# Attention kernel, first attention: score matmuls of 63 and 64 rows, a new step order, and the output norm on ScalarE

## The reference, cut to what matters

```
x: (8, 512, 256) float32; 16 heads of 16; layer norm at its end, no gain or bias
qkv = x @ w_qkv + b_qkv                 # q, k, v: (8, 16, 512, 16)
a = einsum('bhsd,bhtd->bhst', q, k)     # causal: later keys are -inf
a = softmax((a + mask) / sqrt(16))
z = einsum('bhst,bhtd->bhsd', a, v)     # back to (8, 512, 256)
y = layernorm(x + z @ w_out + b_out, eps=1e-5)
```

## Time and profile before

| | us |
|---|---|
| median of 3 runs | 2001.62 |
| lowest, highest run | 1996.41, 2005.23 |
| the profiled execution's own time | 1997.55 |
| its span, first to last instruction | 1996.0 |
| busy in the span: PE, DVE, ACT, POOL | 1787.4, 1109.8, 967.3, 934.7 |
| first attention, to its last matmul | 539.3 |
| of that: seven turns of the loop | 426.1 |

### The profile page before, as it was taken

How to read it: one execution, slowest core, us unless ns; L and a number is a source line. 1 busy time by engine, 2 the same in 40 slices (tenths; PEclk the granted TensorE clock), 3 DMA queues, 4 the chain that set the end, 5 groups by cost and what they waited for, 6 DMA issues and landing times. The chain is left out here.

```text
span 1996.0 us, 42845 instructions
## 1 busy us (share of the span) xinstructions
PE 1787.4 (90%) x14072; PEld 1353.2 (68%) x14072; DVE 1109.8 (56%) x2825; ACT 967.3 (48%) x1898; POOL 934.7 (47%) x923
## 2 busy tenths in 40 slices
PE   5899988898669999999979999599999999789887
PEld 3556655565347777777768888477777777577776
DVE  4566655666467766676523333676676666234343
ACT  2655545554336555555534444265555555333332
POOL 3355444554336655555423333455555555333433
PEclk7898888987779999999979999699999999799998
DMA  4333343334010000000121112100000001121221
GB/s 144 106 115 107 106 122 112 117 109 127 22 33 12 32 32 32 32 32 21 50 58 43 63 63 95 44 12 32 32 32 32 32 21 49 50 70 63 65 74 42
DMA packets 103736, 121.28 MB, mean 61 GB/s; under 512 B 23387, under 2 KB 75781, under 8 KB 103685
## 3 DMA queue, kind: packets, MB, share of 16 engines
q1 hardware_dynamic: 96772, 95.45, 15.7%
q0 software_dynamic: 6912, 25.17, 3.5%
HBM read 82.55 MB, written 37.77 MB: 60 GB/s over the span
## 5 line engine op out<-in xcount | busy, mean ns | idle before, releaser
L468 DVE TENSOR_REDUCE a_negm<-a_x 128x2 f32<-128x256 f32 (+3 forms) x256 | 202.4, 814 | 143.7 <-PE a_x L594 141.5
L430 ACT ACTIVATE a_PT<-a_c 128x384 f32<-128x384 f32 (+1 forms) x384 | 183.7, 522 | 139.7 <-PE a_c L633 84.4
L866 POOL TENSOR_TENSOR work<-work 128x512 f32<-128x512 f32 x128 | 164.5, 1287 | 152.2 <-DVE work L1016 151.0
L1541 DVE SCALAR_TENSOR_TENSOR m_hid<-m_a,mw_b,m_gate 128x512 f32<-128x512 f32 x96 | 71.9, 749 | 244.4 <-ACT m_gate L1479 219.8
L1034 DVE CUSTOM_DVE_ANT_0 l_x<-l_x,window 128x256 f32<-128x256 f32 (+1 forms) x512 | 184.1, 421 | 31.7 <-PE l_x L1131 31.7
L1065 PE MATMUL l_f<-w_hi,tails 128*128 128x512 f32 x384 | 168.8, 440 | 14.2 <-DVE work L1016 11.1
L949 ACT ACTIVATE l_PT<-l_c 128x512 f32<-128x512 f32 (+1 forms) x256 | 125.3, 542 | 87.8 <-PE l_c L1171 84.1
L1436 POOL TENSOR_TENSOR m_hid_lo<-m_hid,m_hid_hi 128x512 fp32r<-128x512 f32 x80 | 102.7, 1291 | 131.3 <-ACT m_hid_hi L1490 131.1
L1066 PE MATMUL l_f<-w_hi,tails 128*128 128x512 f32 x384 | 154.8, 403 | 0.0
L1067 PE MATMUL l_f<-w_lo,tails 128*128 128x512 f32 x384 | 154.1, 401 | 0.0
L880 POOL TENSOR_TENSOR l_PS<-l_PT 128x768 f32<-128x768 f32 x64 | 119.6, 1869 | 58.7 <-ACT l_PT L949 58.7
(11 more groups left out here) (240 smaller groups left out, 5091.8 us busy)
## 6 DMA issues: line engine op xcount, KB each, us to landing
a_Q<-qk_parts SPq DMA_DIRECT2D x192, 64.0 KB, 2.1
a_K<-qk_parts SPq DMA_DIRECT2D x192, 64.0 KB, 2.1
qk_parts<-a_qk_hi SPq DMA_DIRECT2D x32, 256.0 KB, 2.1
qk_parts<-a_qk_lo SPq DMA_DIRECT2D x32, 256.0 KB, 2.2
after_attn<-rows_out POOLq DMA_DIRECT2D x16, 512.0 KB, 5.2
xin<-after_attn SPq DMA_DIRECT2D x32, 256.0 KB, 3.1
m_xr<-after_attn SPq DMA_DIRECT2D x16, 512.0 KB, 4.1
xin<-in_L_attn_x SPq DMA_DIRECT2D x8, 512.0 KB, 3.5
```

The costliest lines, as they stand in the source:

```text
L430: nc.scalar.activation(PT[:, p // PG % 2, 2 * (p % PG) + hh, QOFF[t]:QOFF[t] + nq], SC[hh][:, 0:nq], ACT.Exp, scale=AD ** -0.5).then_inc(e ...
L468: dve.tensor_reduce(negm[:, q, 2 * p:2 * p + 2], MX[i % 2][:, :, 0:nk], AX.X, ALU.max, negate=True).then_inc(max_done, 1)
L866: pool.tensor_tensor(t1[:, par, w, :], t1[:, par, w, :], t2[:, par, w, :], ALU.add)\
```

## The change

1. Rows. The shift row of Q moves from partition 48 to 63 (and 127). The rows between are zero: DVE writes zeros once to 32 partitions at 32 and at 96 of Q, at the start. First-pass score matmuls (sm) read 63 rows in place of 48, second-pass ones (st) 64 in place of 49.
2. Order. STEPS is new. A turn begins at f_x; the three projections f_qk 0 to 2 stand in a row; sm 21 to 26, st 4 to 7 and ms 0 and 1 now belong to the f_ steps and so are done in the turn before (and, for sequence 0, ahead of the loop). The semaphore of the written parts is split in two, one for parts 0 and 1 and one for 2 and 3.
3. Banks. f_qk, mt, pv, f_v and out get new banks, and their waits are rewritten to match.
4. Norm. POOL makes, besides the power, minus the mean times the power (two small instructions more). ACT applies scale and bias in four instructions at step end, in the loop and in the last sequence; the four of POOL and DVE go. POOL keeps the store.

```diff
-        ODD, SLOTS = 64, 48
+        ODD, SHIFT = 64, 63
...
-        QK_IN = [FB[0], FB[1], FB[1], FB[1]]
-        MT_IN = [FB[0], FB[1], FB[0], FB[0]]
-        O_IN = [FB[0], FB[1], FB[1], FB[0]]
+        QK_IN = [FB[1], FB[0], FB[1], FB[0]]
+        MT_IN = [FB[1], FB[0], FB[0], FB[1]]
+        O_IN = [FB[0], FB[1], FB[0], FB[0]]
+        V_IN = [FB[1], FB[0], FB[1], FB[1]]
+        Y_IN = [FB[1], FB[0], FB[1], FB[0]]
...
+            f_x:0 f_xe:0 sm:27 st:8 mt:2 f_qk:0 f_qk:1 f_qk:2 f_qe:0 f_qe:1 f_qe:2 sm:28 st:9 ms:2 sm:29 sm:30
+            f_load:0 st:10 sm:31 st:11 pv:0 st:12 mt:3 ms:3 st:13 z0:0 f_load:1 z1:0 z2:0 f_qk:3 st:14 pv:1 f_sm:0
+            f_qe:3 st:15 ms:4 f_sm:1 f_sm:2 st:16 f_sm:3 st:17 f_sm:4 st:18 f_sm:5 f_load:2 f_sm:6 st:19 f_sm:7 ms:5
+            st:20 z0:1 st:21 f_sm:8 f_sm:9 st:22 z1:1 f_sm:10 f_sm:11 st:23 ms:6 pv:2 z3:0 z2:1 f_mt:0 z0:2 f_load:3
+            f_sm:12 ms:7 z1:2 f_sm:13 pv:3 z3:1 z0:3 z2:2 f_sm:14 f_sm:15 z3:2 f_v:0 z1:3 f_v:1 xr:0 f_v:2 f_st:0
+            f_sm:16 f_mt:1 z2:3 f_st:1 f_sm:17 f_sm:18 f_st:2 f_sm:19 z3:3 f_st:3 f_sm:20 out:0 out:1 out:2 out:3
+            f_sm:21 f_st:4 f_sm:22 f_st:5 f_sm:23 f_ms:0 f_ms:1 f_st:6 end:0 f_sm:24 f_v:3 f_sm:25 f_st:7 f_sm:26
...
-                            at = ODD * hh + SLOTS
+                            at = ODD * hh + SHIFT
...
                     elif name == "out" and i == TB - 1:
...
+                        pool.tensor_scalar(nb[:, :], mv[:, :, 0], -1.0, None, ALU.mult).then_inc(rstd_a, 1)
...
-                        for t in range(TB):
-                            pool.tensor_scalar(out[:, t, :], y[:, t, :], mv[:, t, 0:1], rs[:, t:t + 1],
-                                               ALU.subtract, ALU.mult).then_inc(out_done, 1)
+                        pool.tensor_tensor(nb[:, :], nb[:, :], rs[:, :], ALU.mult).then_inc(rstd_done, 1)
...
+                    elif name == "end":
+                        act.wait_ge(rstd_done, 2 * b + 2)
+                        act.wait_ge(stored, b * 16)
+                        for t in range(TB):
+                            nc.scalar.activation(out[:, t, :], y[:, t, :], ACT.Identity, scale=rs[:, t:t + 1],
+                                                 bias=nb[:, t:t + 1]).then_inc(out_done, 1)
...
+                            for at in (32, ODD + 32):
+                                dve.memset(Q[at:at + 32, :, 0:S].bitcast(F32), 0.0).then_inc(v_set, 1)
...
-                            rows = slice(ODD * hh, ODD * hh + SLOTS)
+                            rows = slice(ODD * hh, ODD * hh + SHIFT)
...
-                            rows = slice(ODD * hh, ODD * hh + SLOTS + 1)
+                            rows = slice(ODD * hh, ODD * hh + ODD)
```

More of the change, by code:

```diff
@@ L193, in first_attention @@
         lo_done, v_done, xhi_done, xlo_done = sem("lo_done"), sem("v_done"), sem("xhi_done"), sem("xlo_done")
-        parts_out = sem("parts_out")
+        parts_out = [sem(f"parts_out{n}") for n in range(2)]
         stacked = [sem(f"stacked{g}") for g in range(AG)]
@@ L216, in first_attention @@
         STEPS = [s.rsplit(":", 1) for s in """
[L217 to L223, removed]
+            f_x:0 f_xe:0 sm:27 st:8 mt:2 f_qk:0 f_qk:1 f_qk:2 f_qe:0 f_qe:1 f_qe:2 sm:28 st:9 ms:2 sm:29 sm:30
[4 more added lines that the diff above has]
+            f_sm:16 f_mt:1 z2:3 f_st:1 f_sm:17 f_sm:18 f_st:2 f_sm:19 z3:3 f_st:3 f_sm:20 out:0 out:1 out:2 out:3
+            f_sm:21 f_st:4 f_sm:22 f_st:5 f_sm:23 f_ms:0 f_ms:1 f_st:6 end:0 f_sm:24 f_v:3 f_sm:25 f_st:7 f_sm:26""".split()]
         STEPS = [(name, int(i)) for name, i in STEPS]
@@ L294, in tail @@
                     if (name, i) == FIRST_OF_LAST:
-                        sp.wait_ge(parts_out, NB * 128)
+                        for n in range(2):
+                            sp.wait_ge(parts_out[n], NB * 64)
                         sp.wait_ge(lo_done, NB * 4)
@@ L500, in do @@
                         dve.wait_ge(y_full, b * TB + i + 1)
-                        dve.tensor_tensor(y[:, i, :], FB[i % 2][:, 0:DM], xr[:, i, :], ALU.add)\
+                        dve.tensor_tensor(y[:, i, :], Y_IN[i][:, 0:DM], xr[:, i, :], ALU.add)\
                             .then_inc(y_done, 1)
@@ L513, in tail @@
                         ahead.low(dve, ahead_raw, ahead_wo, LOW.index((name, i)))
[L514 to L519, removed]
                 steps(dve, do, tail)
@@ L539, in do @@
                         for h in range(KT):
-                            if not isinstance(b, int):
-                                pe.wait_ge(front_free, b * NE - 1 + h)
+                            if not isinstance(b, int) and h == 0:
+                                pe.wait_ge(mrow_done, b * AG - 2)
                                 pe.wait_ge(y_done, b * TB - TB)
+                            elif not isinstance(b, int):
+                                pe.wait_ge(front_free, b * NE)
                             if isinstance(b, int):
@@ L553, in do @@
                         pe.wait_ge(xlo_done, b * KT + KT)
-                        if i > 1:
-                            pe.wait_ge(front_free, b * NE + i)
+                        if i == 1 and not isinstance(b, int):
+                            pe.wait_ge(mrow_done, b * AG - 1)
+                        elif i == 2:
+                            pe.wait_ge(front_free, b * NE + 1)
+                        elif i == 3:
+                            if isinstance(b, int):
+                                pe.wait_ge(front_free, 2)
+                            else:
+                                pe.wait_ge(o_free, b * AG - 3)
                         for h in range(KT):
```

76 lines of the change are left out of this document (39 added, 37 removed).

## The result

| | before | after |
|---|---|---|
| median of 5 runs, us | 2001.62 | 1985.24 |
| lowest, highest | 1996.41, 2005.23 | 1982.06, 1994.36 |
| profiled execution, its own time | 1997.55 | 1994.36 |
| first attention, to its last matmul | 539.3 | 532.7 |

The profiled execution of after happens to be the slowest of its five. A later profile of the same kernel (e5, 1986.46 us) has its last first-attention matmul 5 us earlier: one of its turns takes 58.5 us and not 61.4, and the stretch behind the last f_x is 2.3 us shorter. So what follows is read from places and waits, and sizes are taken from medians.

The account below looks back on a forecast made before the run. PE bounds each turn, with low clock and waits. Rows 4.2 plus removed waits 5.0 minus new waits 3.7 gives 5.5 us a turn, 38.5 in seven; with small terms -40, so 1958 us, range 1926 to 2000.

Parts of the forecast that it names:

- Rows: Score matmuls of the first attention: filled rows, even of zeros, keep PE's clock up, saving 4.2 us a turn.
- I let a fifth of the low time stay: Step in the rows term: some low clock remains after waits, so 5.3 us a turn saved becomes 4.2.
- the sign of being wrong on the rows: What would refute the rows term: score stretches at clock 0.50 with PE busy throughout.
- Waits removed: PE's waits in pv for POOL's masking and ACT's copy, and in the first score step for loads: 5.0 us a turn gone.
- Waits foreseen: New PE waits for ACT: 1.8 us a turn behind the three projections, 1.9 where turns meet, together 3.7.
- the seam: From the last out matmul to the next turn's first projection: PE waits 1.9 us a turn for ACT.
- "1 and 8": Lower and upper bound, in us a turn, on the new waits forecast at 3.7.
- (b): Rival: rows of zeros do nothing for the clock, only removed waits help, 2.1 us a turn: 1984 us, chance 0.15.
- (c): Rival: ACT stands in the norm step waiting for POOL's power, PE idles 5 us where turns meet: 2011 us, chance 0.08.
- (a): Rival: the clock stays up throughout and ACT's new waits are half, 8.5 us a turn saved: 1932 us, chance 0.18.
- the first reading of the prediction: Reading of the profile page: PEclk is 9 in local attention and feed-forward slices, 7 to 9 in the first eleven.
- (d): Rival: the parts of the change cancel without any other rival's mechanism: about 1996 us, chance 0.07.

Follow-up runs that it names:

- e5: The changed kernel run once more, unaltered, beside other runs on one chip: 1984.56 us, 0.9937 of the kernel before.
- e1: The kernel before with only the 63 and 64 rows and their zeros put in: 1985.07 us, 0.9930 of the kernel before.
- e2: The changed kernel with the old 48 and 49 rows and no zeros written: 1998.06 us, 1.0008 of the kernel before.
- e3: The changed kernel with a piece of the weights in Q's rows between, in place of zeros: 1990.92 us, 0.9956 of the kernel before.
- e11: The changed kernel with POOL's add after DVE's last split, and the old 48 and 49 rows without zeros: 1976.29 us, 0.9884 of the kernel before.
- e4: The kernel before, in its old order, with only the output's norm moved to ScalarE: 2031.59 us, 1.0166 of the kernel before.
- e7: The changed kernel without the low part of the output weights, 16 of 32 out matmuls a sequence left out: 1968.03 us, 0.9850 of the kernel before.
- e9: The changed kernel with one wait more, so POOL adds the bias to the residual only after DVE's last output split: 1965.69 us, 0.9833 of before.
- e8: The changed kernel with the low part of the output weights multiplied twice: 1995.56 us, 0.9985 of the kernel before.

## Why the prediction was off

**Rows: mechanism right, size wrong.** Filled rows count for the clock even where they hold zeros (e1, e2, e3). The term was 4.2 us a turn. It measures 12.9 / 8 = 1.6 a sequence in e1, 13.5 / 8 = 1.7 between e2 and e5, and 10.6 / 8 = 1.3 in e11. The step that failed is "I let a fifth of the low time stay": two thirds stay, 10.2 of 15.4 us a turn in e1. The conversion of low time to time was about right: 1.6 us for 5.2 less at the lower level is 0.31, where 4.2 for 12.2 (0.34) was assumed. In e1 the clock still falls behind the wait for pv 0 and over score steps. In the changed kernel, where that wait is gone, it falls all the same: pv 0 takes 4.05 us in four of the seven turns, and 6.8 us of score steps and pv 2 run at 0.50 with PE busy throughout, which the prediction had named as the sign of being wrong on the rows. Turns of 54 to 57 us and a clock over 0.95 didn't come either (60.4 to 61.5 us from the second turn on, 0.90). What it is in the wider reading that raises the clock is not separated: the runs show that 63 and 64 rows do, with zeros or data in them. The Trainium skill, page "TensorE: Matmul & The Clock Gate", section "What's actually happening", ties the level to how busy PE has been; with 63 and 64 rows and the waits all but unchanged the clock in the loop rose from 0.87 to 0.91 in e1, so the trace doesn't agree that busy time alone decides.

**Waits removed: right.** 5.0 us a turn were to go; of them 2.2 / 6 = 0.4 is left, so 4.6 are gone.

**Waits foreseen: right in kind, too large.** For st behind the projections 1.8 us was forecast and (4.8 + 1.9) / 6 = 1.1 measured; for the seam 1.9, and (2.8 + 2.7 + 1.1) / 6 = 1.1. The four norm passes took 2.07 us (e4), between the 1.5 I took and the bound of 2.7, and ACT never idled before them within the loop of the changed kernel. The memsets cost nothing that shows, where 1 was counted. The six sm and four st steps weren't neutral at the ends: the part behind the loop shrank by 5.5. The part ahead of it grew by 1.5, but e7 and e9, with the same program there, have their first f_x at 55.2 and 55.6 us, so that number varies by 3 us between traces.

**The step that cost the forecast: moved steps that got no term.** New waits were looked for in two places, behind the projections and at the seam, and the bounds "1 and 8" were those of these two. The middle of the turn was taken as unchanged. There z1 2 went past pv 3, and with it POOL's add of xr came to lie on DVE's z1 3. The add isn't late for anyone; it is too early. It holds DVE for about 2 us, and DVE's next reduction is what PE waits for, 8.8 / 6 = 1.5 us a turn. Behind that wait the clock falls over out, which e7 and e8 show to be on the path: 5.1 against 3.9 us. Together 1.5 + 1.2 = 2.7 us a turn. The collision comes in six sequences, so that is 16 us; e9 gets back 2.9 a turn and 19 us by medians. With it away, order and norm give 23 us (e11) where 1.3 a turn, 9 in seven, was forecast for waits alone: these two were worth more than forecast, and the collision hid it.

**The sum over again.** Forecast: 4.2 + 5.0 - 3.7 = 5.5 a turn. Measured: 1.6 from rows, 4.6 of waits gone, 2.2 come as foreseen, 2.7 by the collision: 1.3 a turn, 9 in seven, beside the measured 13. This sum is rough, since it mixes medians with the waits of one trace: six turns are 0.4 us a turn shorter than before in the trace of after, and 0.9 in e5's. With one line added the kernel stands at 1965.7, 8 us from the forecast, and that nearness is luck: the rows then give 10.6 us where 4.2 a turn is 29, and order and norm give 23 where 9 was forecast. The two errors cancel.

**The rivals.** (b) named 1984, which is the number measured, for a reason that is wrong, so its nearness is luck: by it e1 would have given nothing and e2 all. (c) is shown as a mechanism by e4, in the old order, but didn't occur in the new order. (a) fell: the clock kept falling. Its ground, and the first reading of the prediction, went too far: the earlier trace rows shows 6 to 8, not 9, in five of the 29 slices behind the first attention. (d) is nearest as a description, for order and norm: e2 is at 1.0008. But it is gain against collision, not gain against the waits that I had listed.

## What to carry to other kernels

When steps are moved, ask of every engine which instructions now run beside each other, not only which run later: here a 2.4 us add of POOL that nobody waited for cost 19 us of 2000, and one wait on a semaphore gave them back. Judge parts of a reordering in the order in which they will run: ScalarE's norm costs 34 us in the old one and gives 9 to 11 in the new one. Look also at what stands right behind each wait: here 3.4 us at the lower clock over the dense matmuls of out cost 1.2 us a turn, nearly as much as the wait of 1.5 us ahead of them.

## What was unexpected of the hardware

POOL holds DVE up. A cast of 0.29 us or a subtraction with two SBUF inputs of 0.42 us took around 2 us more when POOL's add of 1024 elements from SBUF ran, and ended just behind it (2.46 us in the rows above). The Trainium skill has this as a rule, page "SBUF — State Buffer", section "Who interferes with whom": the port pair that VectorE and GpSimd share is an exclusive lock, which a cast in its two-port mode and a subtraction with both inputs in SBUF contend for, and whoever issues first holds it for the whole instruction. The trace agrees: POOL began at 282.54 us and kept its length (2.37 us, before 2.38), and DVE, from 282.74, ended 0.3 us behind it.

Matmuls that read more rows for the same result, rows of zeros, raise the granted clock and save 11 to 13.5 us of 2000; data in those rows gave no more than zeros did. The effect isn't complete: with 63 and 64 rows the clock still went to 0.50 for 10.2 us at a time in e1 while PE was busy throughout.
